# Three rounded passes for the first experts' weights, split during attention, with the matmul and copy orders changed and loops written out

## The chip, the cores and the metric

The kernel runs on one core of one Trainium2 chip, in one launch. The metric is device time in microseconds. Its engines are PE (TensorE; PEld is its weight load, PEq its sequencer), DVE (VectorE), ACT (ScalarE), POOL (GpSimd) and SP (SyncE, which here only issues DMAs).

## The reference, cut to what matters

Sixteen images of 128 channels and 16 x 16 pixels pass an adaptive convolution, a 3 x 3 box sum, and then, as 4096 tokens of 128 channels, four residual layers: softmax attention in each image, a mixture of experts, linear attention, and a second mixture of experts.

```python
    t = t + _L2_attn_ref(_ln_t(t), ...)   
    t = t + _L2_ffn_ref(_ln_t(t), L2_ffn_router_w, L2_ffn_w_gate, L2_ffn_w_up, L2_ffn_w_down)
    t = t + _L3_attn_ref(_ln_t(t), L3_attn_Wq, L3_attn_Wkv)
    t = t + _L3_ffn_ref(_ln_t(t), L3_ffn_Wg, L3_ffn_W, L3_ffn_V, L3_ffn_W2)
```

Each mixture has 8 experts, of which a token uses 2. With x a token, an expert computes

```python
            g = jnp.einsum('sd,edh->esh', flat, w_gate)
            u = jnp.einsum('sd,edh->esh', flat, w_up)
            y = jnp.einsum('esh,ehd->esd', jax.nn.silu(g) * u, w_down)
            out = jnp.einsum('esd,se->sd', y, dense_w)
```

The hidden width h is 256 in the first mixture and 512 in the second.

## The kernel before, in words

The stages follow one another with a barrier between them: adaptive convolution, box sum, softmax attention, `route` and `experts` of the first mixture (tag `d`), linear attention, `route`, `experts` and `combine` of the second mixture (tag `f`). In a stage every engine runs its own instruction list, and semaphores tie the lists together.

**Softmax attention** (`softmax_attention`) works through 16 images, one in each call of `period`. An engine's `period(n)` holds the work on image n and the preparation of images n+1 to n+3. `periods` (L728) writes out images 0 and 1, runs images 2 to 11 as a hardware loop of two images a round, and writes out the last four. On ACT a period ends with `keys(n + 2)` (L816), and the next begins with the exponentials (L830), which wait for PE's scores. On POOL `normed(n + 3)` (L776, L779) is followed by `splits(n + 2)`: `q_low` (L755, waits for the queries), `qa`, `ka`, `kl`, `kb` and the bias sum on T (L771). DVE forms `xT_low` (L1100), which PE's query projection (L893) waits for.

**Routing** (`route`) normalises the tokens into the buffer X, writes them to DRAM, and sorts the 8192 (token, expert) pairs into 71 tiles of 128 slots with one expert each. SP loads the first experts' input weights `w_in` (2 MB) here and `w_out` (1 MB) behind them.

**Experts** (`experts`) does the 71 tiles, software-pipelined. PE's step s, in the order of its list of stages, is:

```python
            pipeline(pe, [(0, gate_up), (-1, load_expert), (-1, transpose_x), (1, transpose_h), (2, down)], SLOT_TILES)
```

So `gate_up` of tile s (L1896 in `d`, L1902 in `f`) is first, then the load of the expert's number for tile s+1 into a register (L1884), the transposition of tile s+1's tokens (L1889), of tile s-1's hidden values (L1910), and `down` of tile s-2 (L1917). ACT's step is `gate` (the silu of tile s, L1934), `copy_x` (the transposed tokens of tile s+1, from PSUM to SBUF, L1938), `copy_h` (tile s-1, L1943). DVE's step is `hidden` (silu times up, L1959) and `result` (y of tile s-2, L1965). In `f` a `low_x` stands before them (L1971).

The two mixtures multiply x by the input weights in different ways. In `d` it is one float32 matmul of 512 columns (gate and up side by side), which PE runs as two instruction records. In `f` weights and tokens are each split in a rounded value (fp32r) and a remainder, and three products of rounded operands are summed, in two halves of 512 columns each: six matmuls. `low_x` makes the tokens' remainder, and PE waits for it through `xg_ready`.

`pipeline` (L119) writes out the first and last steps and runs the rest as a loop of four steps a round, where waits compare with registers; `written_out` (L138) has no loop. In `d` PE runs a `pipeline`, ACT and DVE are written out, because `WeightSplit` uses them to split the `f` weights: a load by SP, a copy on ACT (L1231) and a subtraction on DVE (L1240), 16 pieces, one every four steps.

POOL gathers the token tiles from DRAM by indirect DMA, four buffers deep: the gather of tile k (L1833) waits until tile k-4 is transposed. Results go through four `y` buffers. In `d` SP stores them in the order of slots (L1864). In `f` POOL scatters them (L1839), and its list alternates between one gather and one scatter: the scatter of tile s-2 stands behind the gather of tile s+3.

## Time and profile before

| | |
|---|---|
| median of 3 runs | 954.91 us (952.94 to 957.68) |
| the profiled execution's own time | 959.59 us |
| its span | 957.9 us |
| PE busy | 759.6 us, 79% of the span |
| PEld / DVE / ACT / POOL busy | 580.7 / 528.8 / 469.6 / 438.4 us |
| mean granted PE clock | 0.87 of full speed |
| softmax attention | 128 to 326 us |
| `route` d, `experts` d | 326 to 386, 386 to 528 us |
| linear attention | 528 to 652 us |
| `route` f, `experts` f, `combine` | 652 to 708, 708 to 930, 930 to 958 us |

The profile is of one execution. Times in its rows count from the start of the span. A row of the view by line or by tile gives count, shortest, median and longest duration in ns, and the first and last start in us. In a row of the timeline the first number is the start, the second how long the merged piece lasted, xN the number of instructions, and the bracket the idle time of that engine before it with what ended it. PE durations of neighbouring instructions overlap.

### The profile page before, as it was taken

The page shows a single profiled execution, that of the slowest core. Times are in us where ns is not written, and L with a number is a line of the kernel's source. Part 1 is how long each engine was busy: PE and PEld are TensorE (multiplying, and loading weights), DVE is VectorE, ACT ScalarE, POOL GpSimd, SP SyncE. Part 2 cuts the span into 40 slices and gives each one's busy share as a digit, 9 for nine tenths or more (in the row PEclk, how much of TensorE's full clock was granted, in tenths as well). Part 3 has the DMA queues.
Part 4 walks back from the last instruction along what each step waited for, and adds up shares of the span by engine and source line. Part 5 has one row for each costly group of instructions (what it writes and reads, how often), then busy time and mean ns, then how long its engine had stood idle before and what let it go on. Part 6 is the DMA issues. An engine that isn't in the chain of part 4 may idle for free. (4 is left out here: it accounts for less than half of the span.)

```text
span 957.9 us, 18611 instructions
## 1 busy us (share of the span) xinstructions
PE 759.6 (79%) x4846; PEld 580.7 (61%) x4847; DVE 528.8 (55%) x1510; ACT 469.6 (49%) x1197; POOL 438.4 (46%) x492
## 2 busy tenths in 40 slices
PE   2896968888898756999999056569389999999980
PEld 1675846666665446566666035457358888888870
DVE  6787946777766459344443257764843333333326
ACT  2994435777775324444444156643234444334434
POOL 5000446776772000544443577720026666666744
PEclk9999887999998655999999657985569999999995
DMA  3000000000000140333332121104001111111117
GB/s 98 1 0 20 3 0 2 1 0 0 0 2 1 45 175 2 100 99 99 98 99 62 51 52 47 44 1 176 0 17 37 40 42 44 39 44 40 44 27 263
DMA packets 33165, 45.89 MB, mean 48 GB/s; under 512 B 8115, under 2 KB 22775, under 8 KB 32736
## 3 DMA queue, kind: packets, MB, share of 16 engines
q1 hardware_dynamic: 24256, 27.66, 8.9%
q0 software_dynamic: 8864, 17.72, 7.0%
q8 instruction: 18, 0.29, 0.1%
q14 instruction: 27, 0.22, 0.1%
HBM read 30.21 MB, written 15.60 MB: 48 GB/s over the span
## 5 line engine op out<-in xcount | busy, mean ns | idle before, releaser
L1833 POOL DMA_INDIRECT d_xg<-d_normed,d_gather x71 | 67.2, 946 | 123.6 <-PE ps L1889 66.8
L1094 DVE TENSOR_REDUCE negmax<-ps 128x2 f32<-128x512 f32 x128 | 82.4, 686 | 47.9 <-PE ps L930 47.9
L1833 POOL DMA_INDIRECT f_xg<-f_normed,f_gather x71 | 69.0, 971 | 83.2 <-PEq L1871 58.2
L1934 ACT ACTIVATE f_silu<-ps 128x512 f32<-128x512 f32 x71 | 42.4, 597 | 126.9 <-PE ps L1902 126.9
L1971 DVE TENSOR_TENSOR f_xgT_low<-ps,f_xgT 128x128 fp32r<-128x128 f32 x71 | 20.7, 292 | 144.9 <-ACT f_xgT L1938 144.9
L1839 POOL DMA_INDIRECT f_results<-f_y,f_scatter x71 | 71.9, 1013 | 61.9 <-DVE f_y L1965 53.3
L830 ACT ACTIVATE prob<-ps 128x512 f32<-128x512 f32 x128 | 69.6, 598 | 40.0 <-PE ps L949 40.0
L1896 PE MATMUL ps<-d_w_in,d_xgT 128*128 x142 | 79.5, 642 | 3.9 <-ACT d_xgT L1938 1.5
L1959 DVE TENSOR_TENSOR d_h<-ps,d_silu 128x256 f32<-128x256 f32 x71 | 30.1, 424 | 86.4 <-ACT d_silu L1934 86.4
L1917 PE MATMUL ps<-f_w_out,f_hT 128*128 x568 | 75.2, 275 | 0.6 <-DVE f_y L1965 0.6
L1917 PEld LDWEIGHTS ps<-f_w_out,f_hT 128*128 128x128 f32 x568 | 69.0, 192 | 0.8 <-issue 0.8
L1324 POOL DMA_INDIRECT e_ys<-d_results,d_slots x64 | 60.6, 948 | 18.8 <-issue 18.8
L1934 ACT ACTIVATE d_silu<-ps 128x256 f32<-128x256 f32 x71 | 27.2, 383 | 72.2 <-PE ps L1896 72.2
L1902 PE MATMUL ps<-f_w_high,f_xgT 128*128 x142 | 51.6, 445 | 2.7 <-DVE f_xgT_low L1971 2.7
L947 PE MATMUL ps<-qa,ka 32*128 32x256 f32 x256 | 42.7, 348 | 12.4 <-DVE qb L1104 9.2
L1404 PE MATMUL ps<-ident,e_xn 128*128 128x128 f32 x32 | 8.7, 366 | 54.4 <-DVE e_q L1467 29.4
L1959 DVE TENSOR_TENSOR f_h<-ps,f_silu 128x512 f32<-128x512 f32 x71 | 48.3, 680 | 1.7 <-ACT f_silu L1934 1.7
L1917 PE MATMUL ps<-d_w_out,d_hT 128*128 x284 | 47.6, 290 | 0.6 <-DVE d_y L1965 0.6
L755 POOL TENSOR_SCALAR q_low<-q,lower 128x512 fp32r<-128x512 f32 x16 | 24.9, 1559 | 46.2 <-issue 38.0
L1910 PE MATMUL ps<-ident,f_h 128*128 128x128 f32 x284 | 45.3, 282 | 0.1
L1902 PE MATMUL ps<-f_w_high,f_xgT_low 128*128 x142 | 44.9, 397 | 0.0
L1902 PE MATMUL ps<-f_w_low,f_xgT 128*128 x142 | 44.5, 395 | 0.0
(369 smaller groups left out, 2053.7 us busy)
## 6 DMA issues: line engine op xcount, KB each, us to landing
d_results<-d_y SPq DMA_DIRECT2D x71, 64.0 KB
raw_weights<-in_f_in SPq DMA_DIRECT2D x16, 256.0 KB, 2.9
f_ys<-f_results SPq DMA_DIRECT2D x8, 512.0 KB, 6.4
X<-in_x SPq DMA_DIRECT2D x4, 512.0 KB, 5.8
d_normed<-X SPq DMA_DIRECT2D x8, 256.0 KB, 2.0
d_w_in<-in_d_in SPq DMA_DIRECT2D x1, 2048.0 KB, 7.8
f_normed<-X SPq DMA_DIRECT2D x8, 256.0 KB, 2.0
f_w_out<-in_f_out SPq DMA_DIRECT2D x1, 2048.0 KB, 9.3
```

The source lines that it names most:

```text
L830: nc.scalar.activation(prob[:, h].rearrange("p t q -> p (t q)"), ps[:, h % 2, :], ACT.Exp, scale=SCALE).then_inc(prob_ready, 1)
L947: nc.tensor.matmul(o, ka[rows, b, g, keys], qa[rows, b, g, :], start=True, stop=False)
L1094: nc.vector.tensor_reduce(negmax[:, :, h // HG, col:col + 1], ps[:, 2 + h % 2, :].rearrange("p (t k) -> p t k", t=2), AX_X, ALU.max, negat ...
L1324: nc.gpsimd.indirect_dma_start(ys[:, m % 4, t, c, :], None, moe.y_dram, bass.IndirectOffsetOnAxis(ap=moe.slots[:, c, 2 * m + t:2 * m + t + 1],
L1833: nc.gpsimd.indirect_dma_start(xg[:, n % 4, :], None, moe.xn_dram, bass.IndirectOffsetOnAxis(ap=moe.gather[:, n:n + 1], axis=0)).then_inc( ...
L1839: nc.gpsimd.indirect_dma_start(moe.y_dram, bass.IndirectOffsetOnAxis(ap=moe.scatter[:, n:n + 1], axis=0), y[:, n % 4, :], None, bounds_che ...
L1896: ins = nc.tensor.matmul(ps[:, 2 * at.b, 0:2 * F], xgT[:, at.b, :], of_expert(moe.w_in), start=True, stop=True)
L1902: ins = nc.tensor.matmul(o, x[:, at.b, :], of_expert(w)[:, cols], start=(i == 0), stop=(i == len(passes) - 1))
L1910: ins = nc.tensor.transpose(HT(at.b)[:, c * P:(c + 1) * P], h[:, at.b, c * P:(c + 1) * P], ident[:])
L1917: ins = nc.tensor.matmul(Y(at.b), hT[:, at.b, c * P:(c + 1) * P], moe.w_out[:, bass.ds(expert_of(at), 1), c, :].rearrange("p e c -> p (e c)"),
L1934: nc.scalar.activation(silu[:, at.b, :], GATE(at.b), ACT.Silu).then_inc(silu_ready, 1)
L1959: nc.vector.tensor_tensor(h[:, at.b, :], UP(at.b), silu[:, at.b, :], ALU.mult).then_inc(h_ready, 1)
```

## The change

1. The first experts' `w_in` becomes a rounded half `w_high` and a remainder `w_low`, which live from before attention to the end. Attention loads the 2 MB into X (unused then) and splits them in 16 pieces of 128 x 256: a copy on ACT at the end of each period, and a subtraction on POOL behind it. `route` no longer loads `w_in`.
2. `gate_up` of `d` is three fp32r matmuls of 512 columns. `copy_x` writes fp32r, and DVE gets `low_x` in `d` as well.
3. In both mixtures PE's step starts with `load_expert` and `transpose_x`, and ACT's with `copy_x`, so these now stand ahead of `gate_up` and of the silu. In `d` PE is written out.
4. Eight `y` buffers in both mixtures.
5. Attention is written out on all engines for all 16 images.

```diff
@@ softmax_attention
         def periods(eng, body):
-            for n in range(2):
+            for n in range(N):
                 body(n, n % 2, n)
-            with eng.Fori(0, (N - 6) // 2) as i:
-                for c in (2, 3):
-                    body(2 * i + c, c % 2, None)
-            for n in range(N - 4, N):
-                body(n, n % 2, n)
+
+        @block.sync
+        def _(sp):
+            sp.dma_start(whole, next_dram.rearrange("p e f -> p (e f)")).then_inc(next_in, 16)
...
                 if image_exists(known, 2):
                     splits(n + 2, b)
+                piece = bass.ds(n * PIECE, PIECE)
+                wait_apart(pool, next_high_ready, n + 1, passed_pool)
+                nc.gpsimd.tensor_tensor(whole_low[:, piece], whole[:, piece], whole_high[:, piece],
+                                        ALU.subtract).then_inc(next_low_ready, 1)
 
             periods(pool, period)
+            pool.wait_ge(next_low_ready, N)
...
                 if image_exists(known, 2):
                     keys(n + 2, b)
+                if known == 0:
+                    act.wait_ge(next_in, 16)
+                piece = bass.ds(n * PIECE, PIECE)
+                nc.scalar.activation(whole_high[:, piece], whole[:, piece], ACT.Copy).then_inc(next_high_ready, 1)
@@ route
-            if not moe.split:
-                sp.dma_start(moe.w_in[:], w_in_dram).then_inc(moe.weights_in, 16)
             sp.dma_start(moe.w_out[:], w_out_dram).then_inc(moe.weights_in, 16)
@@ experts
-        xgT = sb("xgT", [P, 2, P], F32R if moe.split else F32)
+        xgT = sb("xgT", [P, 2, P], F32R)
-        y = sb("y", [P, 4, C])
+        y = sb("y", [P, 8, C])
...
-            pe.wait_ge(moe.weights_in, (1 if moe.split else 2) * 16)
+            pe.wait_ge(moe.weights_in, 16)
...
-                if not moe.split:
-                    ins = nc.tensor.matmul(ps[:, 2 * at.b, 0:2 * F], xgT[:, at.b, :], of_expert(moe.w_in),
-                                           start=True, stop=True)
-                else:
-                    passes = ((xgT, moe.w_high), (xgT, moe.w_low), (xgT_low, moe.w_high))
-                    for i, (x, w) in enumerate(passes):
-                        for o, cols in ((GATE(at.b), slice(0, F)), (UP(at.b), slice(F, 2 * F))):
-                            ins = nc.tensor.matmul(o, x[:, at.b, :], of_expert(w)[:, cols],
-                                                   start=(i == 0), stop=(i == len(passes) - 1))
+                outs = ((GATE(at.b), slice(0, F)), (UP(at.b), slice(F, 2 * F)))
+                if 2 * F <= 512:
+                    outs = ((ps[:, 2 * at.b, 0:2 * F], slice(0, 2 * F)),)
+                passes = ((xgT, moe.w_high), (xgT, moe.w_low), (xgT_low, moe.w_high))
+                for i, (x, w) in enumerate(passes):
+                    for o, cols in outs:
+                        ins = nc.tensor.matmul(o, x[:, at.b, :], of_expert(w)[:, cols],
+                                               start=(i == 0), stop=(i == len(passes) - 1))
...
-            pipeline(pe, [(0, gate_up), (-1, load_expert), (-1, transpose_x), (1, transpose_h), (2, down)], SLOT_TILES)
+            stages = [(-1, load_expert), (-1, transpose_x), (0, gate_up), (1, transpose_h), (2, down)]
+            if split:
+                written_out(stages, SLOT_TILES)
+            else:
+                pipeline(pe, stages, SLOT_TILES)
...
-            stages = [(0, gate), (-1, copy_x), (1, copy_h)]
+            stages = [(-1, copy_x), (0, gate), (1, copy_h)]
...
                 if at.reuses:
-                    dve.wait_ge(scattered[at.b4], 16 * at.round)
+                    dve.wait_ge(scattered[at.b8], 16 * at.round)
...
-            low = []
-            if moe.split:
-                dve.sem_inc(xg_ready, 1)
-                low = [(-1, low_x)]
-            stages = low + [(0, hidden), (2, result)]
+            dve.sem_inc(xg_ready, 1)
+            stages = [(-1, low_x), (0, hidden), (2, result)]
```

The order of the instructions at three places (ISA rows are the sequencer's own work on registers and waits).

PE in the first experts, from `gate_up` to the hidden values' transposition, a step of the loop before:

```order
L1893 ISA [waits d_xg_rd]
L1896 ISA [waits d_h_rd]
L1896 MATMUL ps<-d_w_in,d_xgT 128x512
L1884 ISA
L1884 TENSOR_LOAD d_expert
L1887 ISA
L1888 ISA [waits d_gathered2]
L1889 MATMUL ps<-ident,d_xg 128x128 [waits d_xg_rd]
L1907 ISA
L1908 ISA [waits d_h_rd]
L1910 MATMUL ps<-ident,d_h 128x128 [waits d_hT_rd]
```

and a step of the change:

```order
L1896 TENSOR_LOAD d_expert
L1901 MATMUL ps<-ident,d_xg 128x128 [waits d_xg_rd,d_gathered1]
L1913 ISA [waits d_h_rd,d_xg_rd]
L1913 MATMUL ps<-d_w_high,d_xgT 128x512
L1913 ISA
L1913 MATMUL ps<-d_w_low,d_xgT 128x512
L1913 ISA
L1913 MATMUL ps<-d_w_high,d_xgT_low 128x512
L1921 MATMUL ps<-ident,d_h 128x128 [waits d_hT_rd,d_h_rd]
```

The register load and the tokens' transposition moved from behind `gate_up` to ahead of it, and the rows that only compute wait values are gone. In the second experts the same rows move, but the loop and its ISA rows stay.

ACT in the first experts, before:

```order
L1934 ACTIVATE d_silu<-ps 128x256 [waits d_h_rd,d_gu_ps]
L1938 ACTIVATE d_xgT<-ps 128x128 [waits d_xg_ps]
L1943 ACTIVATE d_hT<-ps 128x256 [waits d_y_ps,d_h_ps]
L1231 ACTIVATE f_w_high<-raw_weights 128x512 [waits raw_in1]
L1934 ACTIVATE d_silu<-ps 128x256 [waits d_h_rd,d_gu_ps]
```

and in the change:

```order
L1951 ACTIVATE d_xgT<-ps 128x128 [waits d_xg_ps]
L1947 ACTIVATE d_silu<-ps 128x256 [waits d_h_rd,d_gu_ps]
L1956 ACTIVATE d_hT<-ps 128x256 [waits d_y_ps,d_h_ps]
L1247 ACTIVATE f_w_high<-raw_weights 128x512 [waits raw_in1]
L1951 ACTIVATE d_xgT<-ps 128x128 [waits d_xg_ps]
```

The copy of the next tile's tokens no longer stands behind the silu, which waits for `gate_up`.

POOL in attention, in the change, from the keys' remainder of one period to the queries of the next:

```order
L774 TENSOR_TENSOR kl<-k,ka 128x512 [waits c_kb_rd,c_ka_rd]
L776 TENSOR_SCALAR kb<-kl,upper,one_row 128x512 [waits c_kl_rd]
L780 TENSOR_TENSOR T<-T,bo 128x256 [waits c_xn_rd]
L801 TENSOR_TENSOR d_w_low<-X,d_w_high 128x256 [waits c_next_high]
L785 TENSOR_TENSOR xn_c<-T,ln_mean 128x256 [waits c_xT_ps]
L788 TENSOR_TENSOR xn_c<-xn_c,ln_rstd 128x256 [waits c_centred]
L764 TENSOR_SCALAR q_low<-q,lower 128x512 [waits c_qa_rd,c_q_rd]
```

Only the row L801 is new; the two rows behind it and `q_low` are pushed back by it.

## Rows read from the trace of the kernel before

**Rows 1.** Busy PE, PEld, DVE, ACT, POOL, PE clock, DMA: experts d and f.

```profile
386.00:528.00 142.00, 137.82 (x636) 84.83 (x635) 58.79 (x156) 68.48 (x230) 64.59 (x69) 1.00 0.34 90
...
708.00:930.00 222.00, 218.66 (x1348) 183.87 (x1348) 77.27 (x212) 90.68 (x214) 136.48 (x139) 1.00 0.14 40
```

**Rows 2.** The silu of the first experts by tile: loop steps, then the last written-out ones.

```profile
L1934 ACT ACTIVATE d_silu<-ps x61: 383/383/385, 397.5 to 517.0; 128x256 f32<-128x256 f32 x61
...
L1934 ACT ACTIVATE d_silu<-ps x5: 383/383/384, 518.9 to 526.3; 128x256 f32<-128x256 f32 x5
```

**Rows 3.** Timeline of one step of the first experts, 440.0 to 442.3 us.

```profile
440.15 1.12 PE L1896 MATMUL ps<-d_w_in,d_xgT 128*128 x2
...
441.11 0.27 PE L1889 MATMUL ps<-ident,d_xg 128*128 128x128 f32 x1
...
441.31 0.38 ACT L1934 ACTIVATE d_silu<-ps 128x256 f32<-128x256 f32 x1 [1.12 <-PE ps L1896]
...
441.44 0.66 PE L1917 MATMUL ps<-d_w_out,d_hT 128*128 x4
...
441.59 0.27 ACT L1938 ACTIVATE d_xgT<-ps 128x128 f32<-128x128 f32 x1
...
442.10 0.69 PE L1896 MATMUL ps<-d_w_in,d_xgT 128*128 x1
```

**Rows 4.** The silu of the second experts by tile: the loop's steps.

```profile
L1934 ACT ACTIVATE f_silu<-ps x62: 597/597/600, 724.0 to 911.1; 128x512 f32<-128x512 f32 x62
```

**Rows 5.** Timeline of one step of the second experts, 789 to 795.5 us.

```profile
791.36 0.60 ACT L1934 ACTIVATE f_silu<-ps 128x512 f32<-128x512 f32 x1 [1.83 <-PE ps L1902]
...
791.71 1.06 PE L1917 MATMUL ps<-f_w_out,f_hT 128*128 x8
...
791.85 0.27 ACT L1938 ACTIVATE f_xgT<-ps 128x128 fp32r<-128x128 f32 x1
...
792.16 0.29 DVE L1971 TENSOR_TENSOR f_xgT_low<-ps,f_xgT 128x128 fp32r<-128x128 f32 x1 [2.00 <-ACT f_xgT L1938]
...
792.28 0.97 POOL L1833 DMA_INDIRECT f_xg<-f_normed,f_gather  x1 [0.30 <-issue]
...
792.70 0.73 PE L1902 MATMUL ps<-f_w_high,f_xgT 128*128 x2
...
794.20 0.27 PE L1889 MATMUL ps<-ident,f_xg 128*128 128x128 f32 x1
```

**Rows 6.** PE's sequencer (PEldq) by line: a wait, `down`'s products, register loads, address work.

```profile
L1893 PEldq EVENT_SEMAPHORE  x1: 51/51/51, 520.7 to 520.7; - x1
...
L1917 PE MATMUL ps<-d_w_out,d_hT x4: 275/275/275, 520.9 to 521.2; 128*128 x4
...
L1884 PEldq TENSOR_LOAD <-d_expert x71: 296/302/496, 382.7 to 523.3; - x71
...
L1902 PEldq FUSED_REGOPS  x6: 51/55/60, 792.6 to 793.3; - x6
```

**Rows 7.** The gathered tiles of the second experts: from issue to landing; a later transposition.

```profile
DMA to landing us min/median/max: 2.4/2.5/3.8
...
797.23 0.27 PE L1889 MATMUL ps<-ident,f_xg 128*128 128x128 f32 x1
```

**Rows 8.** Attention: DVE's `heads` by image, loop then written out; ACT, POOL and `xT_low`.

```profile
L1113 DVE TENSOR_TENSOR heads<-ps,inv x12: 423/424/426, 162.9 to 278.7; 128x256 f32<-128x256 f32 x12
L1113 DVE TENSOR_TENSOR heads<-ps,inv x3: 423/425/425, 278.7 to 299.5; 128x256 f32<-128x256 f32 x3
...
201.14 1.08 ACT L830 ACTIVATE prob<-ps 128x512 f32<-128x512 f32 x2 [0.90 <-PE ps L949]
...
203.39 0.73 POOL L771 TENSOR_TENSOR T<-T,bo 128x256 f32 x1
208.02 1.56 POOL L755 TENSOR_SCALAR q_low<-q,lower 128x512 fp32r<-128x512 f32 x1 [2.46 <-issue]
...
L1100 DVE TENSOR_TENSOR xT_low<-xT_c,xT_high x16: 415/466/1259, 132.5 to 289.4; 128x256 fp32r<-128x256 f32 x16
```

More of the change, by code:

```diff
@@ L713, in softmax_attention @@
                                       "out_ps", "bo_added", "tok_rd"))
+        whole, whole_high, whole_low = top.X[:], *(w[:].rearrange("p e f -> p (e f)") for w in halves)
+        PIECE = TOK // N
+        next_in, next_high_ready, next_low_ready = (k.sem(f"c_{s}") for s in ("next_in", "next_high", "next_low"))
         Q = ps[:, 4, :].rearrange("p (g t) -> p g t", g=2)
@@ L1180, with __init__ @@
     SLOT_TILES = (TOP * TOK + E * (P - 1)) // P
-    def __init__(self, nc, k, hidden, tag):
+    def __init__(self, nc, k, hidden, tag, halves=None):
         self.F = hidden
         self.tag = tag
-        self.split = 2 * hidden > 512
-        if self.split:
-            self.w_high, self.w_low = (k.sb(f"{tag}_{s}", [P, self.E, 2 * hidden], F32R) for s in ("w_high", "w_low"))
-        else:
-            self.w_in = k.sb(f"{tag}_w_in", [P, self.E, 2 * hidden])
+        if halves is None:
+            halves = (k.sb(f"{tag}_{s}", [P, self.E, 2 * hidden], F32R) for s in ("w_high", "w_low"))
+        self.w_high, self.w_low = halves
         self.w_out = k.sb(f"{tag}_w_out", [P, self.E, hidden // P, C])
@@ L1198, in __init__ @@
         self.xn_dram = nc.dram_tensor(f"{tag}_normed", [TOK, C], F32, kind="Internal").ap()
-        self.by_slot = not self.split
+        self.by_slot = tag == "d"
         if self.by_slot:
@@ L1848, in _ @@
                     scatter(step - 2)
-            for b in range(4):
-                pool.wait_ge(scattered[b], 16 * ((SLOT_TILES - b + 3) // 4))
+            for b in range(8):
+                pool.wait_ge(scattered[b], 16 * ((SLOT_TILES - b + 7) // 8))
         if moe.by_slot:
@@ L1926, in _ @@
         def _(act):
-            if not moe.split:
-                act.sem_inc(xg_ready, 1)
             act.sem_inc(hT_ready, 2)
@@ L2151, in program @@
             with ExitStack() as first_layer:
-                first = Moe(nc, Kit(nc, first_layer), 256, "d")
-                route(nc, top, first, d["d_router"], d["d_in"], d["d_out"])
+                first = Moe(nc, Kit(nc, first_layer), 256, "d", halves)
+                route(nc, top, first, d["d_router"], d["d_out"])
                 with ExitStack() as side:
```

36 lines of the change are left out of this document (19 added, 17 removed).

## The prediction

> **What bounds the kernel now.** I read the busy time by stretch first, then the silu's starts by tile, which give the experts' step, then the timeline of one step, and last the rows of PE's sequencer and of attention. The chain that ended last covers only the final `combine`, so it says nothing of the stages that change. PE is busy for 137.8 of 142 us in the first experts and 218.7 of 222 us in the second, at full clock [rows 1], yet the steps show that latency sets the pace there, because a busy record lasts until its result has landed.
>
> First experts: the silus of the loop steps start 61 times from 397.5 to 517.0 us, 1.99 us apart. The written-out steps at the end take (526.3 - 518.9) / 4 = 1.85 us [rows 2]. The reader is to see a circle [rows 3]: `gate_up` starts at 440.15, its silu at 441.31, ACT's copy of the next tokens only behind that, at 441.59 to 441.86, though PE transposed them from 441.11 to 441.38, and the next `gate_up` at 442.10. That is 1.95 us: 1.16 + 0.28 + 0.27 + 0.24. The second experts have the same circle with DVE's remainder in it [rows 5]: silu 791.36, copy 791.85, remainder 792.16 to 792.45, `gate_up` 792.70. Their loop step is (911.1 - 724.0) / 61 = 3.07 us [rows 4].
>
> **The change, part by part.**
>
> *The new order (both experts).* The next tokens are transposed ahead of `gate_up`, and copied ahead of the silu. They are then ready about 1 us after a step begins (transposition 0.11 + 0.27, copy 0.27, remainder 0.29) and wanted only at the next. The circle is cut. What is late next is PE's own list.
>
> First experts, array time. One column costs the same in all these products: six rounded matmuls go from 792.70 to 794.20, less about 0.11 for the first weight load, which is 0.23 us each [rows 5]. A step is then 3 x 0.23 for `gate_up` (before, 0.96 - 0.11 = 0.85 us from 440.15 to 441.11 [rows 3]), 0.33 for three transpositions (441.11 to 441.44), and 0.44 for `down`'s four records at the same 0.11: 1.46 us.
>
> Sequencer time. The register load takes 0.30 us, and six address rows in a line start from 792.6 to 793.3, so one takes about 0.13 us [rows 6]. A step of the change has one load, and some nine waits and address rows: 0.36 with its gap + 9 x 0.12 = 1.44 us. That is as long as the array needs, so I add for friction. The sequencer runs ahead: it stood at the next tile's wait at 520.7, before the four `down` products that started from 520.9 to 521.2 [rows 6]. So the load, now at the head of the step, lies beside `down`.
>
> ACT and DVE. ACT has the token copy, 0.27 [rows 3], the silu, 0.38 [rows 2], and a copy of the silu's size; DVE has the remainder, 0.29 [rows 5], a product of the size of `heads`, 0.42 [rows 8], and a copy of the remainder's size. That is about 1.0 each, below 1.46. Every fourth step carries a 128 x 512 piece of the second experts' weights on both, some 0.6 us as that layer's silu [rows 4]; I take half of it as a stall, 0.07 a step. I set the step at 1.56 us. Its ends are 1.46 and 1.80 (the order helps, but the pieces or the sequencer cost 0.3 in each step). Saved: mean now (526.3 - 388.2) / 70 = 1.97; 71 x (1.97 - 1.56) = **29 us** (12 to 36).
>
> Second experts. Array: 6 x 0.23 + 5 x 0.11 + 8 x 0.11 = 2.81 us. The loop stays and its branch costs: in the first experts loop steps are 0.14 us longer than written-out ones [rows 2], though part of that was in the circle. I take 2.88, with ends 2.81 and 3.05 (nothing gained). Saved: 71 x (3.05 - 2.88) = **12 us** (0 to 17), 3.05 being the mean of all 71.
>
> The gather's margin shrinks. The tile issued at 792.28 is transposed at 797.23, 4.95 us later [rows 5, 7]. With the transposition ahead of the 1.50 us of `gate_up`, and two to three shorter steps between, some 3.1 us are left against a landing after 2.5 us (longest 3.8). I take it as covered.
>
> *The split in attention.* Sixteen ACT copies of 128 x 256, about 0.4 us each as the first experts' silu of that size [rows 2], come after `keys`, where ACT waits 0.90 us for the scores [rows 8]. Sixteen POOL subtractions of about 0.73 us (the bias sum of the same size) come where POOL later idles 2.46 us ahead of `q_low` [rows 8]. Both 0. Without that cover they would cost 6 and 12 us. The 2 MB load has the whole first period; `route` loses a load behind which nothing waited. Both 0.
>
> POOL could delay DVE's `xT_low`, for which PE's query projection waits: its rows go from 415 to 1259 ns, median 466 [rows 8], so something holds it at times. The Trainium skill, page "SBUF — State Buffer", section "Who interferes with whom", says that a DVE instruction with two SBUF inputs contends with a GpSimd instruction that reads SBUF, and that the loser blocks for the whole instruction. By that rule 14 images could lose up to 0.6 us each, 8 us; the sum would be 34 instead of 42.
>
> In the trace POOL is already inside its token normalisation when `xT_low` starts, and the subtraction only moves such operations by 0.8 us. I take 0, and 8 us lost as the end.
>
> *Attention written out.* Loop images take (278.7 - 162.9) / 11 = 10.53 us, the written-out ones 10.40 [rows 8]. Ten images leave the loop: **1.3 us** saved. The written-out ones show no stall for code.
>
> *Eight buffers, `down`'s wait.* DVE never waited for a store in these stages. 0.
>
> Sum: 29 + 12 + 1 = 42 us. The profiled execution took 959.6 us and would take 917. It lies 4.7 us above the median of the runs shown, so against 954.9 I forecast **912 us**, 4.5% less.
>
> A rule for the register load speaks against it: the Trainium skill, page "DMA: Bandwidth & Descriptors", section "Latency and other measured facts", gives a `tensor_load` a floor of about 600 ns. By that figure the first experts' step would be 0.3 us longer, and their gain 8 us instead of 29. The trace disagrees with 302 ns, and it decides.
>
> **The rivals.**
>
> *A, the forecast,* 0.70: 900 to 925 us.
>
> *B, half the gain,* 0.18. PE has nothing left to wait for, but ACT, DVE and the sequencer are near 1.4 us a step themselves, and each join costs 0.1 to 0.2. Step 1.80 in the first experts (12 us saved) and 2.97 in the second (6), 1 in attention: 955 - 19 = 936 us. For it: the sum of the sequencer is as long as the array's. Against: the sequencer was seen ahead.
>
> *C, gathers late,* 0.05. If landings of 3.8 us were common, each second-experts step would wait for 0.7 / 2 us: step 3.23, 13 us lost, with 30 gained: 938 us. Against: the median of 2.5.
>
> *D, slower,* 0.04. The register load and its waits are not hidden at the head of the step. Then 0.36 us lie between `down` and the transposition, and of the waits and address rows around it some 0.15 more than the transposition hides: 0.5 us on the array's sum. That gives 1.46 + 0.5 = 1.96 and 2.81 + 0.5 = 3.31: 1 us saved, 18 lost, 1 saved: 971 us. It decides where the sequencer is less than about 0.3 us ahead when `down` ends. Against: 520.7 against 521.2 [rows 6].
>
> *E, it doesn't do what it says,* 0.03: the three passes and the order change nothing because the silu and hidden values' circle is as long, and the POOL subtraction costs 0.6 us an image: 955 us, give or take 5.
>
> **How the numbers follow.** The prediction is A's, 912. The range 900 to 938 holds A and nearly all of B and C, about 0.85 with tails; D and most of E are out. A change of 0.5%, 5 us, is about what a measurement of this kernel can tell from none. Faster by more than that are A, B, C and little of E: 0.93. Within: 0.03. Slower: 0.04.
>
> **What would show it.** In the profile after: silus of the first experts 1.5 to 1.6 us apart, of the second 2.85 to 2.95; ACT's copy of tokens starting before the silu, within 0.1 us of the transposition's end; three records of 0.23 us spacing in `gate_up`; the register load running beside `down`; attention's images 10.4 us apart, with ACT's wait for the scores shrunk from 0.9 to about 0.5 us and POOL's ahead of `q_low` from 2.5 to 1.6. A step above 1.75 us with PE idle ahead of the transposition speaks for D, ahead of it for a gather for C, and an attention image above 10.6 us for the held `xT_low`.

## The result, and the profile after

| | before | after |
|---|---|---|
| median, same chip | 953.92 us (950.24 to 957.68, 4 runs) | 913.05 us (911.91 to 921.17, 4 runs) |
| ratio | | 0.959, 95% interval 0.952 to 0.966 |
| the profiled execution's own time | 959.59 us | 911.91 us |
| its span | 957.9 us | 910.2 us |

Forecast: 912.0 us in a range of 900 to 938. The medians differ by 40.9 us, the profiled executions by 47.7. Ratios, here and below, compare the executions in the faster of a kernel's two states, both kernels on the same chip, so they can differ by up to 1% from the quotient of the medians beside them. Three rows by tile and line show where most of this went (count, shortest, median and longest duration in ns, first and last start in us):

```profile
L1947 ACT ACTIVATE d_silu<-ps x71: 383/383/385, 378.6 to 489.0; 128x256 f32<-128x256 f32 x71
...
L1947 ACT ACTIVATE f_silu<-ps x71: 597/599/599, 674.6 to 878.0; 128x512 f32<-128x512 f32 x71
...
L1131 DVE TENSOR_TENSOR heads<-ps,inv x16: 424/424/426, 164.1 to 315.8; 128x256 f32<-128x256 f32 x16
```

To be seen: the first experts' step is (489.0 - 378.6) / 70 = 1.58 us (before 1.97), so 70 steps take 27.8 us less than the 138.1 between the first and last silu of before [rows 2]. The second experts' step is (878.0 - 674.6) / 70 = 2.91 us (before 3.05), 10.1 us less. From the last silu of the first experts to the first of the second it is 185.6 us, as before (185.9). What is left are 9.6 us ahead of the first silu, 388.2 us before and 378.6 after. They lie at attention's end and in the stages behind it, and most of them are not the change's: the `heads` of the 14th image start at 299.5 us before and at 299.3 after. The windows of the same 28 us in both kernels (busy PE, PEld, DVE, ACT, POOL, granted PE clock, DMA share, GB/s), before:

```profile
303.00:331.00 28.00, 21.93 (x128) 12.04 (x129) 10.00 (x34) 8.15 (x15) 1.11 (x7) 0.57 0.01 2
```

and after:

```profile
303.00:331.00 28.00, 21.22 (x186) 14.60 (x186) 15.65 (x55) 12.23 (x25) 2.58 (x9) 0.94 0.16 57
```

The granted clock was 0.57 in one execution, mostly at the lower level of 1.2 GHz, and 0.94 in the other, mostly at 2.4 GHz. From 299 to 303 us it is 1.00 in both, with PE busy for 2.70 of the 4 us in both; from 303 to 307 it is 0.54 in the one and 1.00 in the other. The last two of attention's `heads` came 12.05 and 10.31 us after the ones ahead of them in before, 8.94 and 7.62 us after the change: 5.8 us. The experiments below take up whose these are.

The windows of the two stages of experts, after:

```profile
375.00:491.00 116.00, 114.18 (x708) 95.07 (x706) 72.66 (x228) 74.46 (x230) 72.92 (x69) 1.00 0.42 112
670.00:882.00 212.00, 209.12 (x1347) 181.10 (x1346) 89.03 (x212) 98.06 (x214) 136.46 (x138) 1.00 0.15 42
```

PE's busy share is as high as it was (98% and 99%; 97% and 98% in [rows 1]), and its weight loads now fill 82% and 85% of the time, against 60% and 83%. That second share tells what the first hides: the array gets work closer together (in the first experts a step also has one weight load more, ten instead of nine). ACT, DVE and POOL are at 42 to 64%.

One step of the first experts (the timeline; in brackets the idle time before, and what ended it):

```profile
419.47 0.61 PE L1928 MATMUL ps<-d_w_out,d_hT 128*128 x4
...
419.92 0.27 PE L1901 MATMUL ps<-ident,d_xg 128*128 128x128 f32 x1
419.98 0.50 PE L1913 MATMUL ps<-d_w_high,d_xgT 128*128 x1
...
420.23 0.28 ACT L1951 ACTIVATE d_xgT<-ps 128x128 fp32r<-128x128 f32 x1
420.32 0.39 PE L1913 MATMUL ps<-d_w_low,d_xgT 128*128 x1
420.41 0.68 DVE L1256 TENSOR_TENSOR f_w_low<-raw_weights,f_w_high 128x512 fp32r<-128x512 f32 x1
...
420.55 0.40 PE L1913 MATMUL ps<-d_w_high,d_xgT_low 128*128 x1
...
420.99 0.38 ACT L1947 ACTIVATE d_silu<-ps 128x256 f32<-128x256 f32 x1 [0.48 <-PE ps L1913]
421.00 0.61 PE L1928 MATMUL ps<-d_w_out,d_hT 128*128 x4
421.01 0.28 DVE L1984 TENSOR_TENSOR d_xgT_low<-ps,d_xgT 128x128 fp32r<-128x128 f32 x1
...
421.45 0.29 PE L1901 MATMUL ps<-ident,d_xg 128*128 128x128 f32 x1
421.67 0.49 PE L1913 MATMUL ps<-d_w_high,d_xgT 128*128 x1
```

The circle is cut: ACT copies the next tile's tokens at 420.23, 0.76 us ahead of the silu, where before the copy stood behind it [rows 3]. The transpositions come 1.53 us apart. The piece of DVE at 420.41 (a part of the second experts' weights, every fourth step) pushes the remainder `xgT_low` from the end of ACT's copy at 420.51 to 421.01, and `gate_up`, which needs it, comes at 421.67, 1.69 after the last one. From `gate_up` to `gate_up`, the 15 steps of the steady part in which DVE starts such a piece take 1.60 to 1.72 us (mean 1.66), the 15 in which ACT copies one 1.56 to 1.65 (1.62), and the 35 with neither 1.49 to 1.63 (1.54). From silu to silu the shortest steady step is 1.47.

PE's sequencer, in the same step and over the whole stage:

```profile
L1896 PEldq TENSOR_LOAD <-d_expert x2: 296/304/312, 419.3 to 420.9; - x2
...
L1900 PEldq EVENT_SEMAPHORE  x70: 51/51/51, 376.6 to 486.3; - x70
```

The register load for the next tile starts at 419.3, before `down` of this step begins at 419.47: it is hidden beside it, and 302 ns before the change are 300 ns after it (medians of 71) [rows 6]. Beside the load a step has nine wait and address rows, as many as the prediction counted.

### The profile page after: what moved, and what is told of

It is laid out like the page before. It is cut to its first block and busy times, and to the rows that moved or that the text cites. A ratio compares the mean times of both kernels' runs of the same rounds, so it can differ in the third digit from the quotient of the medians.

```text
span 910.2 us, 18314 instructions
## 1 busy us (share of the span) xinstructions
PE 713.8 (78%) x4917; PEld 579.8 (64%) x4918; DVE 552.7 (61%) x1581; ACT 488.5 (54%) x1213; POOL 459.4 (50%) x508
## 5 line engine op out<-in xcount | busy, mean ns | idle before, releaser
L1845 POOL DMA_INDIRECT d_xg<-d_normed,d_gather x71 | 75.2, 1059 | 85.2 <-PEq L1883 50.7
L844 ACT ACTIVATE prob<-ps 128x512 f32<-128x512 f32 x128 | 69.6, 598 | 32.6 <-PE ps L967 32.6
L1972 DVE TENSOR_TENSOR d_h<-ps,d_silu 128x256 f32<-128x256 f32 x71 | 30.2, 425 | 32.6 <-ACT d_silu L1947 31.4
L965 PEld LDWEIGHTS ps<-qa,ka 32*128 32x128 f32 x256 | 25.8, 191 | 29.6 <-DVE qb L1122 12.5
L1928 PE MATMUL ps<-d_w_out,d_hT 128*128 x284 | 43.5, 276 | 0.6 <-DVE d_y L1978 0.6
L342 PE MATMUL ps<-fcol,wimg 128*128 (+1 forms) x160 | 40.3, 399 | 3.8 <-DVE wimg L432 3.1
L1921 PE MATMUL ps<-ident,f_h 128*128 128x128 f32 x284 | 42.7, 273 | 0.1
```

What stands on the lines that cost most here:

```text
L342: last = nc.tensor.matmul(ps[:, 2 + b, a * PIX:(a + 1) * PIX], wimg[:, a, t, :], rhs.rearrange("p n r c -> p (n r) c"), start=(t == 0), st ...
L844: nc.scalar.activation(prob[:, h].rearrange("p t q -> p (t q)"), ps[:, h % 2, :], ACT.Exp, scale=SCALE).then_inc(prob_ready, 1)
L965: nc.tensor.matmul(o, ka[rows, b, g, keys], qa[rows, b, g, :], start=True, stop=False)
L1845: nc.gpsimd.indirect_dma_start(xg[:, n % 4, :], None, moe.xn_dram, bass.IndirectOffsetOnAxis(ap=moe.gather[:, n:n + 1], axis=0)).then_inc( ...
L1921: ins = nc.tensor.transpose(HT(at.b)[:, c * P:(c + 1) * P], h[:, at.b, c * P:(c + 1) * P], ident[:])
L1928: ins = nc.tensor.matmul(Y(at.b), hT[:, at.b, c * P:(c + 1) * P], moe.w_out[:, bass.ds(expert_of(at), 1), c, :].rearrange("p e c -> p (e c)"),
```

## The experiments

Most are single edits of the change or of the kernel before; the deeper gathers and linear attention each build on the kernel ahead of them. Of longer edits only the main lines are shown. They ran in three groups on three chips: the kernel before took 956.58 us on the first (median of 15 runs), 1004.74 on the second (13 runs, one of them 2392 us, which the ratios leave out), 991.95 on the third (11 runs). So only the ratio to before, and the steps of the profiles, compare across the groups.

### First group: which part of the change carries the gain

**The old order, with everything else of the change**

```diff
-            stages = [(-1, load_expert), (-1, transpose_x), (0, gate_up), (1, transpose_h), (2, down)]
+            stages = [(0, gate_up), (-1, load_expert), (-1, transpose_x), (1, transpose_h), (2, down)]
...
-            stages = [(-1, copy_x), (0, gate), (1, copy_h)]
+            stages = [(0, gate), (-1, copy_x), (1, copy_h)]
```

> The changed kernel with PE's and ACT's old stage orders in both experts (gate_up ahead of the next tile's transposition, silu ahead of the token copy); everything else of the change stays. Theory S (the new order cut a circle of latencies, and that is where the gain is): the circle comes back and is longer than before in the first experts, because DVE's remainder now lies in it: 1.85 (written-out step of before) - 0.16 (shorter gate_up) + 0.31 (remainder) = 2.00 us a step against 1.58 in the changed kernel; second experts back to 3.0 to 3.07. Time about 913 + 71 x (0.42 + 0.13) = 952 us. Rival P (the cheaper rounded passes and the written-out lists bring the gain): first experts 1.70, second 2.9, time about 922 us.

Measured: 952.37 us, ratio 0.999 (0.994 to 1.005).

```profile
L1947 ACT ACTIVATE d_silu<-ps x71: 384/384/386, 377.5 to 518.6; 128x256 f32<-128x256 f32 x71
...
L1947 ACT ACTIVATE f_silu<-ps x71: 597/597/601, 704.9 to 918.5; 128x512 f32<-128x512 f32 x71
```

Steps of 2.02 and 3.05 us. Three rounded passes, PE written out and eight buffers bring nothing while the circle stands. Against before's written-out steps of 1.85 us [rows 2], `gate_up` is 0.16 us shorter on the array (0.69 for 0.85), and the remainder on DVE, now between ACT's copy and `gate_up`, adds about 0.3.

**The new order alone, in the kernel before**

```diff
-            pipeline(pe, [(0, gate_up), (-1, load_expert), (-1, transpose_x), (1, transpose_h), (2, down)], SLOT_TILES)
+            pipeline(pe, [(-1, load_expert), (-1, transpose_x), (0, gate_up), (1, transpose_h), (2, down)], SLOT_TILES)
...
-            stages = [(0, gate), (-1, copy_x), (1, copy_h)]
+            stages = [(-1, copy_x), (0, gate), (1, copy_h)]
```

> The kernel before with the new stage orders of PE and ACT in both experts and nothing else: float32 gate_up in the first experts, PE's loops, four result buffers, attention as before. Theory S: first experts limited by PE's array at 0.85 + 0.33 + 0.44 = 1.62 us plus what the loop costs, 1.75 a step (before 1.97), second 2.91 (before 3.05): 954 - 16 - 10 = 928 us. If PE's sequencer with its loop rows is what limits (about 5 rows of 0.12 more than written out, so 1.3 + 0.6 = 1.9): first experts 1.9, 939 us. Rival P: no gain, 954 us.

Measured: 940.69 us, ratio 0.983 (0.979 to 0.987).

```profile
L1934 ACT ACTIVATE d_silu<-ps x71: 383/383/385, 387.7 to 519.0; 128x256 f32<-128x256 f32 x71
...
L1934 ACT ACTIVATE f_silu<-ps x71: 597/599/599, 704.4 to 908.2; 128x512 f32<-128x512 f32 x71
```

In the second experts the order is the whole gain: 2.91 us, as in the change. In the first it gives 1.88 us, a quarter of the 0.39 us. The circle is cut here too. What is late next is not the array, which would need 1.62 us by the sum in the expectation; the next kernel shows what it is.

**The change, with PE of the first experts as a loop**

```diff
-            if split:
-                written_out(stages, SLOT_TILES)
-            else:
-                pipeline(pe, stages, SLOT_TILES)
+            pipeline(pe, stages, SLOT_TILES)
```

> The changed kernel with PE of the first experts as a loop of four steps again. Theory Q (PE's sequencer is as long as the array in the changed kernel, and the loop adds some five wait and address rows of 0.12 us a step): first experts about 2.0 us a step instead of 1.58, 943 us. Rival (the sequencer is hidden, the loop costs only its branch, 0.14 a step as in before): 1.72, 923 us.

Measured: 945.28 us, ratio 0.996 (0.987 to 1.005).

```profile
L1944 ACT ACTIVATE d_silu<-ps x71: 384/384/386, 389.0 to 530.0; 128x256 f32<-128x256 f32 x71
```

The step is 2.01 us. So in the first experts PE's list has to be written out: in the loop its sequencer computes a wait's value or an address in a row of its own, about 0.12 us from one to the next, for each wait and each pass. Twenty steps of the loop have 14 such rows each where the written-out list has nine, and three passes have more of them than the one product they replace (12 rows and 1.88 us a step in the kernel above). The three address rows of one `gate_up` last 51 ns or less but start from 431.1 to 431.4:

```profile
L1913 PEldq FUSED_REGOPS  x3: 46/51/51, 431.1 to 431.4; - x3
```

The timeline of that kernel shows PE's transposition waiting for nothing but issue:

```profile
430.91 0.32 PE L1901 MATMUL ps<-ident,d_xg 128*128 128x128 f32 x1 [0.39 <-issue]
```

Taken together: without the order nothing (2.02), with the order and a loop nothing (2.01), with the order, the written-out list and the three passes 1.58. The order and the written-out list don't add up; each is worth little until the other has taken its bound away. Order and written-out code with the one float32 product was not tried. So what the three passes bring, and with them the split in attention, is not shown: by the array's sum it is at most 0.16 us a step, 11 us.

**Four result buffers instead of eight**

```diff
-        y = sb("y", [P, 8, C])
+        y = sb("y", [P, 4, C])
```

> The changed kernel with four result buffers instead of eight in both experts. Theory: a result has 4 x 1.58 = 6.3 us until its buffer is needed again and a store lands within some 3 us, so nothing changes: 913 us, no wait of DVE for a store. Rival: the faster steps need the eight buffers; DVE waits for stores in the first experts, step 1.7 or more, 922 us or more.

Measured: 919.58 us, ratio 0.961 (0.955 to 0.966), which overlaps the change's. Steps of 1.58 and 2.90 us, as with eight. The buffers carry nothing that these runs can tell. Its profile has the low clock at attention's end, though, with attention's code the same as in the change:

```profile
303.00:331.00 28.00, 21.30 (x142) 11.93 (x141) 11.67 (x40) 9.65 (x19) 2.57 (x9) 0.66 0.05 19
```

The granted clock is 0.66, the last two images came after 9.83 and 10.30 us, and the first silu at 387.7 us. The profile with the old order, also with this attention, has 0.94, 8.94 and 7.62 us, and 377.5 us, as the change; the one with PE's loop, again with this attention, has 0.63 and 389.0 us.

### Second group: PE's list alone, and what else could be moved

**PE in the new order, ACT in the old**

```diff
-            stages = [(-1, copy_x), (0, gate), (1, copy_h)]
+            stages = [(0, gate), (-1, copy_x), (1, copy_h)]
```

> The changed kernel with ACT's old order in both experts (silu ahead of the next tile's copy) and PE's new one. Theory S says that the circle runs through ACT's order: the copy of tile n+1 waits behind the silu of tile n, so the circle is whole again and PE gains nothing by its early transposition, which even lengthens it (the next transposition must wait for the remainder): transposition 0.1, gate_up with its landing 0.9, silu 0.28, copy 0.31, remainder 0.31, sequencer 0.25: 2.1 us a step in the first experts, 3.1 in the second: about 913 + 71 x (0.52 + 0.2) = 964 us. Rival (PE's order is what counts, ACT's is a detail): 1.6 and 2.9, 913 us.

Measured: 1009.54 us, ratio 1.004 (1.000 to 1.007), and a step of (535.0 - 376.9) / 70 = 2.26 us in the first experts, the slowest of all.

```profile
431.74 0.38 ACT L1947 ACTIVATE d_silu<-ps 128x256 f32<-128x256 f32 x1 [1.42 <-PE ps L1913]
...
432.02 0.27 ACT L1951 ACTIVATE d_xgT<-ps 128x128 fp32r<-128x128 f32 x1
...
432.32 0.29 DVE L1984 TENSOR_TENSOR d_xgT_low<-ps,d_xgT 128x128 fp32r<-128x128 f32 x1 [1.43 <-issue]
...
432.76 0.30 PE L1901 MATMUL ps<-ident,d_xg 128*128 128x128 f32 x1 [0.40 <-DVE d_xgT_low L1984]
...
432.99 0.49 PE L1913 MATMUL ps<-d_w_high,d_xgT 128*128 x1
```

The circle is back, and 0.24 us longer than with both old orders (2.02): PE's transposition now stands inside it, between the remainder (its PSUM buffer comes free there) and `gate_up`. That is more than the 2.1 us expected. The second experts' step is 3.48 us (3.1 expected), on a chip where it is long in every kernel, as the next ones show. The two halves of the order are worth something only together; one half alone costs.

**The register load behind `gate_up`**

```diff
-            stages = [(-1, load_expert), (-1, transpose_x), (0, gate_up), (1, transpose_h), (2, down)]
+            stages = [(-1, transpose_x), (0, gate_up), (-1, load_expert), (1, transpose_h), (2, down)]
```

> The changed kernel with the register load of the expert's number behind gate_up again, in both experts. Theory Q: the load only takes sequencer time, and as much behind gate_up as ahead of the transposition, since the sequencer is ahead of the array at both places: first experts 1.55 to 1.60, second 2.89 to 2.92, 913 us. Rival D of the prediction (at the head of the step the load is not hidden): the first experts fall to 1.5 or less, the second to 2.83, 902 us.

Measured: 969.26 us, ratio 0.964 (0.957 to 0.972). The first experts' step is 1.60 us, between 1.58 in the first group and 1.62 in the next kernel. The place of the load makes no difference that these steps can tell.

**PE of the second experts written out too**

```diff
-            if split:
-                written_out(stages, SLOT_TILES)
-            else:
-                pipeline(pe, stages, SLOT_TILES)
+            written_out(stages, SLOT_TILES)
```

> The changed kernel with PE of the second experts written out as well (ACT and DVE keep their loops). Theory: the array needs 2.83 us a step there, and what is above it (2.91 measured) is PE's branch every fourth step, about 0.1, and late gathers. Written out, 2.86 a step, 910 us. If gathers are what limits: unchanged, 2.90, or the waits grow since the other steps are shorter, 913 us.

Measured: 966.20 us, ratio 0.961 (0.953 to 0.969), not told apart from the kernel ahead of it. Its second experts' step is 3.42 us, far above 2.91, and so it is (3.43) with the loop. On this chip something else sets it. Most steps take 2.8 to 3.6 us, but 13 of 70 take more than 5 us, followed by short ones. In the timeline of one:

```profile
811.50 0.59 ACT L1953 ACTIVATE f_hT<-ps 128x512 f32<-128x512 f32 x1
...
812.39 0.33 PE L1901 MATMUL ps<-ident,f_xg 128*128 128x128 f32 x1
...
814.30 0.29 DVE L1975 COPY f_y<-ps 128x128 f32<-128x128 f32 x1 [1.97 <-remote]
814.33 0.28 ACT L1948 ACTIVATE f_xgT<-ps 128x128 fp32r<-128x128 f32 x1 [2.24 <-remote]
```

ACT should have copied the tokens once PE had them, at about 812.7, and DVE the result of `down` at about 812.3. Both start 0.03 us apart, nearly 2 us late, while PE goes on (`remote` stands where the profile shows nothing that released the wait).

**The same, with gathers five tiles ahead in eight buffers**

```diff
-        xg = sb("xg", [P, 4, C])
+        xg = sb("xg", [P, 8, C])
...
-            for step in range(-3, SLOT_TILES + 2):
-                if step + 3 < SLOT_TILES:
-                    gather(step + 3)
+            AHEAD = 5
+            for step in range(-AHEAD, SLOT_TILES + 2):
+                if step + AHEAD < SLOT_TILES:
+                    gather(step + AHEAD)
```

> The kernel with PE written out in both experts, and the gathers in both five tiles ahead into eight buffers instead of three tiles ahead into four. Theory G (in the second experts the early transposition has used up the gather's margin: lead 3.05 us against a landing of 2.6 and more, and one late gather cost 1.4 us): no step waits for a gather, 2.84 a step, 908 us. Rival (the gathers were in time, the extra is the loops of ACT and DVE): as the kernel without deeper gathers, 2.86 to 2.90.

Measured: 971.82 us, ratio 0.967 (0.959 to 0.975). In the second experts most transpositions now follow their gather by 8 to 12 us, and PE waits for none of them but at the stage's start. Without the deeper gathers it waited 16 times, 8.0 us in all. The step is still 3.41 us. The long steps of this chip are not late gathers alone. (In its first experts one step takes 8.15 us, with no cause found, and lifts the mean to 1.72; the median is 1.58.)

### Third group: attention's loop, and more written out

**Attention's loop put back into the change**

```diff
-            for n in range(N):
-                body(n, n % 2, n)
+            for n in range(2):
+                body(n, n % 2, n)
+            with eng.Fori(0, (N - 6) // 2) as i:
+                for c in (2, 3):
+                    body(2 * i + c, c % 2, None)
+            for n in range(N - 4, N):
+                body(n, n % 2, n)
```

> The change, with attention's loop of two images a round put back (the split of the weights stays). Theory: writing attention out is worth only the loop's own 0.13 us an image: images of the loop 10.5 us apart instead of 10.39, 1.3 us in all, and the split in it costs nothing, so the total is that of the change plus 1 to 2 us, a ratio of 0.960 to 0.962 to before where the change has 0.959. The profile's 9 us less ahead of the first experts came from the matmul clock at attention's end, which should be seen high or low in either form. Rival 1, the loop hid a cost of the split: images above 10.7 us, 3 us or more lost. Rival 2, it is the written-out form that keeps the clock high at attention's end: then this profile has the clock low at 303 to 330 us and the last two images at 12 and 10.3 us, and the total is 6 to 9 us above the change's, a ratio near 0.967.

Measured: 965.06 us, ratio 0.974 (0.967 to 0.980), beside 0.972 for the change on the same chip. The loop's images are 10.47 us apart, the written-out ones of the next kernel 10.40: 0.7 us for ten. The window of attention's end reads

```profile
303.00:331.00 28.00, 21.68 (x170) 14.18 (x162) 13.72 (x48) 11.53 (x23) 1.84 (x8) 0.81 0.13 48
```

another value of the clock, with the last images after 9.89 and 8.92 us and the first silu at 379.4. So an early start does not need the written-out form. Whether the form changes how often the clock stays high is not settled: of the profiles here, none of three with the loop has 0.94 (0.57, 0.59, 0.81), and six of eleven written-out ones have.

**All engines of the second experts written out**

```diff
-                pipeline(act, stages, SLOT_TILES)
+                written_out(stages, SLOT_TILES)
...
-                pipeline(dve, stages, SLOT_TILES, 8)
+                written_out(stages, SLOT_TILES, 8)
```

and PE's list as above.

> The change, with the second experts written out on PE, ACT and DVE as well. Theory: what is left between the second experts' step of 2.91 us and the array's 2.83 is the loops' branches and address rows: step 2.83 to 2.85, 4 to 5 us off, and on a chip where the loop steps stall (the profiles of the second batch show ACT and DVE standing for 2 us together once in four steps, with a step of 3.4 us) 40 us off. Rival 1, gathers: with 3.05 us from gather to transposition and landings of 2.5 to 3.5 us, the step stays at 2.9 and the total changes by less than 1 us. Rival 2, the stall is not the loops' but one of fetching instructions in any form: the step stays at 3.4 on such a chip.

Measured: 954.47 us, ratio 0.961 (0.955 to 0.967), against 965.70 us and 0.972 (0.967 to 0.978) for the change on this chip: 11 us less at the median, with intervals that just touch. The next kernel, with the same experts, lies at 0.966. That is 0.6 to 1.1% less than the change, so likely faster on this chip, but not clear of noise.

```profile
L1944 ACT ACTIVATE f_silu<-ps x71: 592/599/619, 689.0 to 918.0; 128x512 f32<-128x512 f32 x71
```

Its step is (918.0 - 689.0) / 70 = 3.27 us; with the change's second experts it is 3.46 (in the kernel with attention's loop) and 3.41 (in the change, below) on the same chip. Part of the excess is the loops': the median step falls from 3.40 to 2.94. Steps of 4.7 us and more are as many as before, 16 of 70 against 15 and 13, so loops are not all of it: between the theory's 2.85 and the rival's 3.4. PE also waits for gathers more often, 15 times and 7.9 us in all against 3 times and 1.7 us with attention's loop. Deeper gathers were not tried in this form, and this form not on a chip with steps of 2.91 us.

**Linear attention written out as well**

```diff
-            pipeline(act, [(-1, transposed), (-3, norm_factors), (-2, normed), (0, parts)], N, 4)
+            written_out([(-1, transposed), (-3, norm_factors), (-2, normed), (0, parts)], N, 4)
```

and the same for PE and DVE.

> The change with the second experts written out on all three engines, and the loops of linear attention (ACT, PE and DVE) written out too. Theory: linear attention's step is not set by PE's array; if its loops cost what attention's did, 0.13 us an image, the gap from the last silu of the first experts to the first of the second goes from 185.6 to 184 us, 2 us off; on a chip where loop steps stall, where the gap is 197 to 203 us, some 10 us off. Rival: this stage waits for DMA and DVE, the gap stays within 1 us.

Measured: 954.68 us, ratio 0.966 (0.960 to 0.971). The gap between the two mixtures' silus is 198.4 us with it and without it. The rival was right, nothing is gained.

**The change once more**

> The change itself once more, to stand beside the other three on the same chip. Expected: a ratio of 0.959 to before (0.952 to 0.966), steps of 1.58 and 2.91 us; the matmul clock at attention's end is high in one execution and low in another of the same code, which moves the first experts' start between 378 and 388 us. Rival: the start stays at 378 with the change and at 388 with the kernel before, so that it belongs to the code.

Measured: 965.70 us, ratio 0.972 (0.967 to 0.978), which just misses the 0.966 that closed the interval of the first measurement: on this chip the change gives 26 us, not 41. Its profile is of an execution of 976.27 us, the longest of the six. The window of attention's end reads

```profile
303.00:331.00 28.00, 22.33 (x133) 12.91 (x125) 10.46 (x35) 9.36 (x17) 1.84 (x8) 0.61 0.06 20
```

with the last images after 12.05 and 10.31 us and the first silu at 387.4 us, as in the kernel before (0.57, the same two gaps, 388.2). The same code started its first experts at 378.6 us in the profile after the change. So the rival is out: the start does not belong to the code alone.

The first experts have the same step within 0.04 us on every chip (1.58 to 1.62, in the kernels that keep the change's order, list and gathers). The second experts' is 3.41 here where the first chip had 2.91. The kernel before was not profiled on the two slower chips, so how much longer its own steps are there is not known.

## Why the prediction was right

**The circle and what follows it.** Right, and carried by the runs. The first experts' step was to be 1.56 us and is 1.58; the term was 29 us and measured 27.8 over 70 steps. That the bound is then PE's own list shows in the weight loads' share and in the shortest step of 1.47, beside 1.46 added up from the array. Which part of that list, is not told apart: the array's sum is 1.46 us and the sequencer's 1.44, and the steps with no piece in them still take 1.54. The stall from the weights' pieces was taken as 0.07 us a step, and it is 0.05: (0.12 + 0.08) / 4 from the means of 1.66 and 1.62 against 1.54. One of the named signs came otherwise: the three records of `gate_up` start 0.34 and 0.23 us apart (419.98, 420.32, 420.55), not 0.23 each.

**The second experts.** The term was 12 us (step 2.88) and measured 10.1 (2.91). Many steps are 2.83 us, where 2.81 was added up. The longer ones are mostly of two kinds that the term did not have apart: those in which PE's loop branches, every fourth, of which most take 2.98 to 3.33 us from `gate_up` to `gate_up` (median 3.06), and two that wait for a gather. A chip with steps of 2.91 never ran the written-out form, so that the branch itself costs this is argued, not shown.

**The gather's margin.** I took 3.1 us from issue to transposition, and it is 2.95 to 3.5 in most steps (median 3.21), against a landing of

```profile
DMA to landing us min/median/max: 2.4/2.6/3.5
```

"Covered" was nearly right: PE sat idle for a gather twice, for 0.97 and 0.27 us. The first,

```profile
838.35 0.97 POOL L1845 DMA_INDIRECT f_xg<-f_normed,f_gather  x1 [1.84 <-DVE f_y L1978]
...
841.00 0.32 PE L1901 MATMUL ps<-ident,f_xg 128*128 128x128 f32 x1 [0.97 <-DMA f_xg<-f_normed,f_gather]
```

came where POOL itself was late: the gather stood behind a scatter that stood behind DVE's result. A lead of 4.95 us [rows 5, 7] would have covered such a delay. Rival C did not come, but the margin it spoke of is spent.

**The split in attention.** Sixteen copies and sixteen subtractions, as sized (0.4 and 0.73 us):

```profile
L889 ACT ACTIVATE d_w_high<-X x16: 413/414/417, 158.2 to 311.9; 128x256 fp32r<-128x256 f32 x16
...
L801 POOL TENSOR_TENSOR d_w_low<-X,d_w_high x16: 719/726/734, 162.1 to 312.5; 128x256 fp32r<-128x256 f32 x16
```

They cost nothing: the images are 10.40 us apart, as the written-out ones were before [rows 8], and POOL's idle time ahead of `q_low` fell from 2.46 us to the 1.64 of this row (1.6 was foretold):

```profile
208.58 1.56 POOL L764 TENSOR_SCALAR q_low<-q,lower 128x512 fp32r<-128x512 f32 x1 [1.64 <-issue]
```

ACT's wait for the scores of an image in the middle fell from 0.90 to 0.52 us (about 0.5 was foretold), so it too was paid from idle time. (Over all of attention it fell from 40.0 to 32.6 us, which holds the different ends too.) The 8 us that the rule of the Trainium skill (page "SBUF — State Buffer", section "Who interferes with whom") would have taken did not come:

```profile
L1118 DVE TENSOR_TENSOR xT_low<-xT_c,xT_high x16: 415/415/583, 131.6 to 289.2; 128x256 fp32r<-128x256 f32 x16
```

In every image but the first the subtraction ended about 0.6 us before `xT_low` began (204.69 + 0.72 = 205.41, and 206.05), so the two never met. But `xT_low` meets other POOL operations, and there the trace agrees with the rule: the one that comes second lasts longer. Before:

```profile
136.79 1.26 POOL L759 TENSOR_TENSOR qa<-q,q_low 128x512 fp32r<-128x512 f32 x1
137.08 1.26 DVE L1100 TENSOR_TENSOR xT_low<-xT_c,xT_high 128x256 fp32r<-128x256 f32 x1 [4.17 <-ACT xT_high L805]
...
204.95 0.61 POOL L779 TENSOR_TENSOR xn_c<-xn_c,ln_rstd 128x256 f32<-128x256 f32 x1 [0.25 <-POOL xn_c L776]
...
205.38 0.47 DVE L1100 TENSOR_TENSOR xT_low<-xT_c,xT_high 128x256 fp32r<-128x256 f32 x1
```

and after:

```profile
206.05 0.41 DVE L1118 TENSOR_TENSOR xT_low<-xT_c,xT_high 128x256 fp32r<-128x256 f32 x1
206.16 0.77 POOL L788 TENSOR_TENSOR xn_c<-xn_c,ln_rstd 128x256 f32<-128x256 f32 x1 [0.18 <-POOL xn_c L785]
```

The row of 1259 ns is `xT_low` standing behind `qa`, which ended at 138.05: 0.84 us on top of the 0.42 it takes alone, while 0.97 us of `qa` were left. In ten images before, it took 0.46 to 0.60 us because POOL's second normalisation step had begun first. After the change that step is 0.8 us later and begins second: `xT_low` takes 0.42, and POOL's step 0.77 or 0.78 us in ten images instead of 0.61. So the one in second place waits for most of what is left of the first, 0.84, 0.05 and 0.16 us longer here, and the change moved the small waits from DVE to POOL, which had idle time. That the price is 0 was right, in part by luck: that POOL's shifted operations would meet `xT_low` the other way round was not foreseen. The long first wait is not the change's to save: the longest `xT_low` is 583 ns in the profile after, and 1257 in that with four result buffers, which has the same attention.

**Attention written out.** 1.3 us foretold from 10.53 and 10.40 us. The images of the change are 10.40 apart, so the term holds against before; the loop put back into the change cost 0.7 us of the profile, which the times can't tell from nothing.

**The register load.** 0.30 us and hidden, as taken; moving it behind `gate_up` changed nothing. Rival D's mechanism is not there. The 600 ns of the Trainium skill (page "DMA: Bandwidth & Descriptors", section "Latency and other measured facts") was no price for this load in any trace here.

**Where the sum was met by more than its terms.** 29 + 12 + 1 = 42 us (954.9 less 42 is 912.9; the forecast says 912), and the medians give 40.9. The steps and attention's 1.3 us account for 39.2. The profiled executions differ by more, 47.7, and the rest of that difference is mostly the clock at attention's end, which a reading of two profiles alone would have given to the change. The prediction took off 4.7 us because the profiled execution lay above the median; that is probably a part of the same thing: on the first chip the 15 executions of the kernel before go from 941.53 us, at a mean granted clock of 0.895, to 959.85 us, at 0.874.

**What the prediction did not see.** Of the loop it said that its steps "are 0.14 us longer than written-out ones [rows 2], though part of that was in the circle", and put PE's written-out list into the sum without a price of its own. The run with the loop shows that price: 2.01 against 1.58 us a step, 30 us, as much as the order's. Had the change left the loop in place, the same working, which counted only nine waits and address rows, would have been 30 us wrong. What the passes bring beside the order and the list was not priced apart either, and no run does so. Nor did it see that the gain depends on the chip: 41 us on one, 26 on another.

## What to carry to other kernels

Find the circle first (a product, its consumer, the copy that feeds the next product), and take what the next round needs out of it on every engine at once; on one engine alone it can make the circle longer. Then add up the sequencer's rows of the engine that becomes the bound, not only its array time: where both are near the same, a loop's computed waits and addresses can eat the whole gain, and written-out code is a part of the change, not a finish. Before a difference between two profiles is explained, look whether a third one of the same code shows it.

## What the runs showed of the hardware

The granted clock at attention's end differs between executions of the same attention code (0.94 and 0.66 over 303 to 331 us, and 0.61 for the change run again), and the first silu behind it moves by 9 us with it (378.6, 387.7 and 387.4 us). What decides it was not tried.

The sequencer of PE needs about 0.12 us from one wait or address row to the next while the rows themselves show 0.05 us; in the loop of the first experts, with 14 such rows a step instead of nine, that added 0.43 us to a step whose array work is 1.46.

Where DVE's subtraction `xT_low` and a POOL operation overlap, the second to begin is longer by what is left of the first, less about 0.13 us (0.84 for 0.97 us left, 0.05 for 0.18, 0.16 for 0.30).

Two of three chips had a second experts' step of 3.3 to 3.5 us instead of 2.91, in part from steps in which ACT, or ACT and DVE together, start some 2 us late while PE goes on. Deeper gathers don't remove it (3.41), written-out code removes a part (3.27 for 3.41 to 3.46). Its cause stays open.
